# Attention in a macaron block: the exponential moved behind the next group's first copy in ScalarE's order

## The reference, cut to what matters

```python
x = query                                     # 8 x 1024 x 256, float32
x = x + 0.5 * ffn(layernorm(x))               # FP4-rounded, 256 -> 704 -> 256
x = x + attention(layernorm(x))
x = x + 0.5 * ffn(layernorm(x))

def attention(x):                             # 16 heads of 64, causal
    q, k, v = heads(x @ Wq), heads(x @ Wk), heads(x @ Wv)
    w = softmax(q @ k.T / 64 + causal)
    w = w * mask(span_val)                    # a factor for each head and key
    w = w / (sum(w) + 1e-8)
    return (w @ v) @ Wo
```

## Time and profile before

| what | value |
|---|---|
| median of 3 runs | 3453.69 us (3452.92 to 3454.66) |
| the profiled execution | 3454.41 us, its span 3452.6 us |
| granted TensorE clock, mean | 0.983 of full speed |
| attention's loop in the trace | about 600 to 2937 us |
| pairs in it | 64, mean 36.5 us |

### The profile page before, as it was taken

One profiled execution on the slowest core, in us unless ns is written; L12 is line 12 of the kernel. 1 busy time (PEld: TensorE's weight loads), 2 busy tenths in 40 slices (PEclk: granted clock), 3 DMA queues, 4 the chain that ended last, 5 costly groups with the idle time before them and its releaser, 6 DMA issues.

```text
span 3452.6 us, 76458 instructions
## 1 busy us (share of the span) xinstructions
PE 3223.7 (93%) x28848; PEld 2677.1 (78%) x28848; DVE 2967.2 (86%) x5704; ACT 2367.8 (69%) x4315; POOL 845.1 (24%) x910
## 2 busy tenths in 40 slices
PE   4999996999999999999999999999999999799998
PEld 4999994677777777777777777777777777699998
DVE  8999984888888888888888888888888888899996
ACT  3666653777777777777777777777777777466664
POOL 2344321222222122222122222122222122233331
PEclk8999998999999999999999999999999999899999
DMA  3133312222323233222233223223222323111110
GB/s 108 60 98 89 103 39 66 61 56 67 91 51 70 62 80 71 63 75 67 54 78 79 57 65 85 58 56 99 59 55 63 78 62 117 34 54 56 56 55 31
DMA packets 160348, 235.74 MB, mean 68 GB/s; under 512 B 30064, under 2 KB 71152, under 8 KB 159728
## 3 DMA queue, kind: packets, MB, share of 16 engines
q1 hardware_dynamic: 159984, 230.84, 25.4%
HBM read 95.49 MB, written 34.61 MB: 38 GB/s over the span
## 4 chain that ended last, share of the span: by engine, by line
PE 42%; DVE 17%; issue 16%; ACT 7%; POOL 2%; DVEq 0%; ACTq 0%; POOLq 0%
DVE at_e_rows L1550 8%; PE ffn_gu_ps L505 7%; PE at_side_ps L1295 7%; PE at_t_ps L1377 6%; PE at_o_ps L1393 5%; DVE at_eT_lo L1556 4%; ACT at_eT_hi L1466 4%; PE ffn_down_ps L530 4%; PE at_s_ps L1366 3%; PE at_s_ps L1367 3%; PE at_side_ps L1344 3%; PE at_side_ps L1307 1%; DVE at_v_masked L1528 1%; PE ffn_hT_ps L475 1%; DVE at_oT_lo L1514 1%
## 5 line engine op out<-in xcount | busy, mean ns | idle before, releaser
L1556 DVE SCALAR_TENSOR_TENSOR at_eT_lo<-at_t_ps,at_eT_hi 128x512 f16<-128x512 f32 (+3 forms) x1536 | 852.4, 555 | 268.6 <-ACT at_eT_hi L1466 246.7
L1458 ACT ACTIVATE at_e_rows<-at_e_rows,at_neg_max 128x1024 f32<-128x1024 f32 (+7 forms) x1024 | 791.5, 773 | 321.3 <-DVE at_neg_max L1550 319.3
L1466 ACT ACTIVATE at_eT_hi<-at_t_ps 128x512 f16<-128x512 f32 (+3 forms) x1536 | 742.8, 484 | 158.3 <-PE at_t_ps L1377 144.7
L1550 DVE CUSTOM_DVE_ANT_0 at_e_rows<-at_s_ps,at_strip,keep_s_scale 128x1024 f32<-128x1024 f32 (+7 forms) x1024 | 827.7, 808 | 7.0 <-PE at_s_ps L1367 6.2
L1377 PE MATMUL at_t_ps<-at_ident,at_e_rows 128*128 128x128 f32 x4608 | 802.5, 285 | 1.8
L1393 PE MATMUL at_o_ps<-at_v_cols,at_eT_hi 128*128 128x132 f16 x4608 | 611.3, 222 | 10.1 <-ACT at_o_raw L1477 6.4
L1393 PE MATMUL at_o_ps<-at_v_cols,at_eT_lo 128*128 128x66 f16 x4608 | 568.6, 193 | 0.0
L1366 PE MATMUL at_s_ps<-at_kh_st,at_q_st 128*128 128x512 f16 (+3 forms) x1536 | 502.2, 327 | 18.3 <-DVE at_acc L1540 12.5
L1377 PEld LDWEIGHTS at_t_ps<-at_ident,at_e_rows 128*128 128x128 f32 x4608 | 493.8, 141 | 7.1 <-ACT at_e_rows L1458 6.5
L1393 PEld LDWEIGHTS at_o_ps<-at_v_cols,at_eT_hi 128*128 128x128 f16 x4608 | 433.6, 97 | 79.2 <-DVE at_eT_lo L1556 15.7
L1367 PE MATMUL at_s_ps<-at_kl_st,at_q_st 128*128 128x512 f16 (+3 forms) x1536 | 481.9, 327 | 0.0
(11 more groups left out here) (219 smaller groups left out, 6576.9 us busy)
## 6 DMA issues: line engine op xcount, KB each, us to landing
at_kh_st<-at_k_hi SPq DMA_DIRECT2D x256, 128.0 KB, 2.3
at_kl_st<-at_k_lo SPq DMA_DIRECT2D x256, 128.0 KB, 2.4
at_w_qk<-w_qk_split SPq DMA_DIRECT2D x65, 256.0 KB, 3.0
at_q_st<-at_q_hi SPq DMA_DIRECT2D x128, 128.0 KB, 2.4
at_q_st<-at_q_lo SPq DMA_DIRECT2D x128, 128.0 KB, 2.4
at_w_v<-w_v_split SPq DMA_DIRECT2D x66, 128.0 KB, 2.4
ffn_x_rows<-in_L_attn_query_dram SPq DMA_DIRECT2D x32, 256.0 KB, 3.2
ffn_x_res<-in_L_attn_query_dram SPq DMA_DIRECT2D x32, 256.0 KB, 3.7
```

The source lines that it names most:

```text
L1458: nc.scalar.activation(e_rows[:, n % 4, :w], e_rows[:, n % 4, :w], ACT.Exp, bias=neg_max[:, n % 4:n % 4 + 1], scale=-1.0).then_inc(sem("ex ...
L1466: nc.scalar.activation(eT[0][:, i % EBUF, :count * P], t_ps[i % TBUF][:, :count * P], ACT.Copy, scale=PSCALE).then_inc(sem("eT_hi"), 1)
L1550: nc.vector.tensor_tensor_reduce(e_rows[:, n % 4, :w], s_ps[n % 2][:, col:col + w], strip[:, SEQ - w:], keep["s_scale"][:, 0:1], BIGGEST, ...
L1556: nc.vector.scalar_tensor_tensor(out=eT[1][:, i % EBUF, :count * P], in0=t_ps[i % TBUF][:, :count * P], scalar=PSCALE, in1=eT[0][:, i % EB ...
```

## The change

`pair_steps` no longer appends the step `exp` at the end of the first group of a unit. It keeps it in a list `late_exp`, which is emptied right behind the next group's `turn`, and after the last group of the pair. Only ACT carries out `exp`, so only ACT's list changes: the exponential changes places with the copy-out (if one is due) and the copy of group i+1 that used to follow it. A piece's high part at group i+1 follows both before and after. At the end of a pair the exponential of group 23 stays where it was.

```diff
-    steps, late_lo = [], []
+    steps, late_lo, late_exp = [], [], []
...
             steps.append(("turn", i, 0))
+            flush(late_exp)
             if i or before:
                 steps.append(("lo", (i - 1) % NG, (i - 1) // NG))
             flush(late_lo)
...
             if first and more:
-                steps.append(("exp",) + unit)
+                late_exp.append(("exp",) + unit)
...
     flush(late_lo)
+    flush(late_exp)
```

## The result

The changed kernel takes 3474.4 us (median of 4 runs, 3472.6 to 3476.9) against 3453.3 for the kernel before beside it: ratio 1.0064, 95% interval 1.0050 to 1.0079, so 21 us or 0.6% slower. The forecast was 31 us slower. The profiled execution took 3472.6 us with a span of 3470.8, 18.2 more than the span before.

What follows compares the result with a forecast made beforehand. PE, 93% busy, was taken to be bound by its few real stops, not DVE's waits. Terms 21.3 + 5.8 + 6.4 - 2 = 31.5 us on 3453.7 gave 3485; stated range 3442 to 3510.

Steps and rivals of the forecast that it cites:

- The rival that DVE's waits are the path: Relieved DVE waits come back to PE at the wo and v pieces: 28.5 us faster, 3425; chance 0.20.
- Step A: End of each pair: late copy-out delays PE's value of group 21 by 0.38 us at 56 boundaries, 21.3 us.
- Step B: Plain even pairs: late copy-out at group 15 and smaller losses, less a wo stop: 0.32 us each, 18 pairs, 5.8 us.
- the copy-out term: Plain even pairs: PE's value of group 15 starts at 1871.25 instead of 1870.71, 0.54 us lost.
- the wo stop: Plain even pairs: PE's stop of 0.47 us in front of the second wo piece goes, as DVE empties the bank earlier.
- Step C: Odd pairs: late second k piece and turns of groups 20 and 14, less a v stop: 0.20 us each, 32 pairs, 6.4 us.
- the k piece: Odd pairs, group 7: high part of the second k piece comes 0.33 us late, and this lands on PE.
- The rest: Odd pairs: turn of group 20 loses 0.22 us, turn of group 14 0.1; the last v piece's stop absorbs 0.45.
- Step D: Other even pairs: seven row pairs gain 0.3 us each, about 2 us; seven turning pairs come out at 0.
- no difference: Smaller losses and gains cancel, and the pair-end stop comes out of the next pair's q-piece waits: 3454; chance 0.12.
- nothing absorbed: Stops in plain even and odd pairs shift the pieces meant to absorb them: 56 us slower, 3510; chance 0.10.
- the signs named: ACT's minimum waits and DVE's copy waits more than halve; PE's copy-out waits grow to 50 or 75 times, 20 to 30 us.

Runs made afterwards that it cites:

- chosen set: Kernel before with exponentials moved only behind group 12, behind 15 in odd and turning pairs, behind 18 in odd pairs, and all in row pairs: 3412.9 us.
- all but group 21: Changed kernel with the exponential behind group 21 put back ahead of the copy of group 22 and the copy-out: 3449.0 us, ratio 0.9993 to the kernel before.
- groups 0 to 11: Kernel before with only the exponentials behind groups 0 to 11 moved, eight of sixteen: 3461.4 us, ratio 1.0025.
- the experiment on groups 5, 6 and 17: Kernel before with the exponentials behind groups 5, 6 and 17 moved, in odd pairs only: 3465.4 us in a single run.
- the last two kernels of the table: The chosen set, 3412.9 us, and the same with exponentials behind groups 0 to 11 also moved in the first odd pair of each sequence, 3411.4 us.

## Why the prediction was right, and where its terms were off

- **The sign and the mechanism** were right: relieving DVE's waits brings PE only what its few stops hold, and PE then stops at the output bank. The rival that DVE's waits are the path is refuted twice: the changed kernel and the chosen set leave as much of them (174.1 and 172.4 us) and lie 61 us apart, and "all but group 21" leaves the least (135.5) and is no faster than the kernel before.
- **Step A**: forecast 0.38 at 56 boundaries, measured 0.46 (undone: every interval 0.46 less, 25 us in all). The 0.08 is in the main the hand-over: the sum went from the copy-out's end at 1879.56 to the value at 1879.60, 0.04, while after the change it is 0.14 from 1885.64 + 0.38 = 1886.02 to 1886.16. The other links of the chain came out within 0.02 each.
- **Step B**: the copy-out term, 0.54 forecast, is 0.61 alone. The second half of a plain pair without step A is 36.24 - 35.97 = 0.27 longer (all but group 21, less groups 0 to 11); forecast 0.54 + 0.15 - 0.47 = 0.22. That the wo stop would go is borne out (18.3 to 2.5). The first half of such a pair, put at 0.1 for the copy-out at group 5, is 0.03 longer (I with groups 0 to 11 moved).
- **Step C**: the k piece costs 0.30 alone and 0.17 with the whole first half moved, forecast 0.33. The 0.13 between them is at the second q piece, in front of which PE had a stop that DVE's gain takes away. The forecast's list of PE's stops leaves the q pieces out, though they were the second largest line of side pieces (29.0 us before, 23.7 after). The rest, 0.22 + 0.10 - 0.45 = -0.13, is measured as 36.35 - 36.49 = -0.14, and the experiment on groups 5, 6 and 17 shows the absorption itself.
- **Step D failed in size**, for the odd pair behind the row pair and for the clock. I gave the row pairs -0.3 each and let the odd pair behind them pay 0.33 for its k piece as any other, about 0 for interval R. Measured it is -0.8 to -1.4, and with the shorter one of the first sequence -8.2 us in all (the seven intervals of before sum to 274.93, those of after to 266.76). The row pairs themselves brought about 3.1 us against the 2 forecast. The odd pairs behind them brought 2.8, where they were to lose 2.3: DVE is still behind there, and every relieved wait counts (38.92 against 38.48, the last two kernels of the table). The clock brought about 2.2, for which the forecast has no term.
- **The total** is nearer than its terms, by luck. Step D's miss of 8 us stands for most of the 10 between the forecast of 31 and the measured 21. Step A was 4 to 5 us too small (56 x 0.08) and step C about 4 too large (25 odd pairs x 0.16), and these two cancel.
- **The rivals** of no difference and of nothing absorbed: the first is refuted by step A's interval, the second by the run on groups 5, 6 and 17.
- **Of the signs named**: the copy-out's waits were forecast at 50 to 75 and 20 to 30 us and are 86 and 31.8: 55 at the boundaries, 24 at group 15 in the 18 plain pairs and in six of the row pairs, and 7 in the first and last pairs. The forecast did not see those in the row pairs. The turns' wait for exponentials was to gain 6.4 us and gained 8.1 (6.5 to 14.6). ACT's wait for the minimum fell by far more than half, DVE's for the copy by less than a third.

## What to carry to other kernels

Moving an instruction back in an in-order queue delays it and also everything that now stands behind it for as long as what it was put behind has not arrived: list each successor with the time at which its consumer needs it; in this kernel the cost was the copy-out, which had 0.42 us of slack and came 0.74 later (its end 1.94 us behind the turn's start instead of 1.20). The most waited-for line of the table (308 us here) told nothing of the gain here; the stops of the engine that has no other holes did, and a set of moves picked by them gave 38 us where moving everything lost 21. Where a kernel repeats to a hundredth of a microsecond, intervals between like instructions show single terms that totals hide.

## What was not expected of the hardware

Behind PE stops of 2.08 us the granted clock fell to its lower level for most of the next 4 us, at four of six places in each of five kernels (20 of 30 stops); behind stops of 1.46 us, at the same places of five other kernels, it fell at none of 30. Each is one profiled execution. A fall cost 0.55 to 1.37 us of the interval here. What decides between the four and the two, and whether the length of the stop is what counts, these runs don't show. From the end of ACT's copy-out to PE's first value matmul 0.14 us pass, from the end of an exponential to the first transpose 0.05.
